# Local attention: probabilities turned by VectorE and DMA, values read by token, and a rotation's two products in one instruction

## The chip, the cores and the metric

The kernel runs on one core of one Trainium2 chip. The time is device microseconds (us) of one execution; lower is better. The core has TensorE (PE; its weight loads are shown apart as PEld), VectorE (DVE), ScalarE (ACT), GpSimd (POOL) and SyncE (SP, which here only issues DMA copies). Each engine works through its own queue in order, and they meet through semaphores.

## The reference, cut to what matters

x is 2 sequences of 1024 tokens with 128 channels. A recurrent mixing layer comes first (the first 317 us of the kernel; not touched here). Then come 6 layers of windowed attention and a gated feed-forward, with 16 heads of 64 and windows of 32 tokens:

```
def attn_layer(x, Wqkv, qs, ksc, Wo):
    q, k, v = split_heads(x @ Wqkv)
    q = l2norm(q) * qs;  k = l2norm(k) * ksc
    q = q * cos * scale + rotate_half(q) * sin * scale      # rotate_half: concat(-x2, x1)
    k = k * cos / scale + rotate_half(k) * sin / scale
    # window w of 32 queries looks at the 64 keys of windows w-1 and w
    sim = einsum('bhwie,bhwje->bhwij', bq, bk2) * 8.0
    out = einsum('bhwij,bhwje->bhwie', softmax(mask(sim)), bv2)
    return out @ Wo
```

## The kernel before, in words

The 2048 tokens are 16 blocks of 128, and 6 layers give a stream of 96 blocks, n = 0 to 95 (`STREAM`). Everything is float32 except the mask. `stream(turn)` runs 96 turns; in turn t each engine runs the stages of `turn(at, pair)` in the order in which its own `turn` function lists them. `at(lag, stage)` runs a stage for block t - lag. `pair(lag, stage)` runs a stage for a pair of two blocks, only in every other turn. So several blocks are in flight, and the order on each engine is written out by hand (lines 1307, 1479, 1668, 1832).

Two kinds of turn alternate. In an odd turn PE runs, beside the attention, `project_o` (16 matmul records of 256 columns), most of the feed-forward's matmuls and `centres`; in an even turn only `variances` and `up_gate_full`. They are called the long and the short turn below.

What a block goes through:

- `project_qk` (L1342) makes q and k in four parts of 512 columns in PSUM: q in banks 1 and 2, k in banks 0 and 1. `project_v` (L1347) makes v in two parts: part 0 in bank 2, part 1 in bank 0. Each therefore waits until the q or k part that held its bank has been read. The `rotated` semaphore says so: `rotate(n, i)` adds 3 for each part i (12 for a block), and `project_v(n, i)` waits for `6 + 3 * i`: part 0 needs rotations 0 and 1, part 1 needs rotations 0 to 2.
- `square` (ACT, L1582) squares each part; `norms` (DVE, L1768) sums the squares by head.
- `rotate(n, i)` (DVE, L1758 and L1762) multiplies part i by the cosines (512 columns into `qk`) and, in two instructions of 256 columns that cross the halves of each head, by the sines (into `turnedhalf`). GpSimd's `add_turned` (L1280) adds the two, `unit` (L1286) multiplies by the inverse norms.
- Two turns later PE turns k and q (`turn_k`, `turn_q`, L1355), ACT reads them from PSUM (L1610, L1604), PE makes the scores in banks 4 and 5 (L1390), DVE does `peaks` and `shifts` (L1774, L1781), ACT the exponential, DVE the `totals` and their reciprocals (L1788, L1790), GpSimd the division `unit_probs` (L1304).
- In the turn after that PE turns the probabilities (`turn_p`, 8 transposes of 128x128 into banks 6 and 7), ACT copies them to `p_T` (`read_p`, L1622), and PE makes the outputs (L1417) from `v_win` and `p_T` into banks 4 and 5, which ACT reads (`read_o`, L1629).
- `v_win` holds for each window the 64 value rows that it needs: `place_v` (SP, L1229 and L1231) fills it with 16 copies of 64 KB for each block.

SP also loads the next layer's weights (`load_layer`, L1207), 4 times within the stream, after `place_v` of a layer's seventh block. PE's order in a turn: `project_v(.., 1)` of the block before, `turn_k`, `turn_q`, `project_qk` 0 and 1, masks and scores, `turn_p`, (`down`), `project_qk` 2 and 3, `project_v(.., 0)`, (`project_o`), `outputs`, (`centres`). DVE's order: (`gated_full`), rotation 0, (`norm_x`), (`gated_tail`), rotation 1, `peaks`, `shifts`, (`add_ffn`), `norms` 0, rotations 2 and 3, `totals`, (`add_attention`), `norms` 1. Stages in brackets run in every other turn.

Of the kernel before, what the change touches and what calls it, by code (L numbers as in the profile page):

```python
# [28 lines left out]
P = 128  # L29
# [11 lines left out]
AH = 16  # L41
# [1035 lines left out]
LAG = 6  # L1077
PAIR = 2
# [3 lines left out]
V_SLOTS = 3  # L1082
# [4 lines left out]
def build_stream(nc, a, sems, ctx, banks, x, x_mid, early, mixed, out):  # L1087
# [49 lines left out]
    rotated, rot_added, ss_made, above_floor = sig("rotated", per=12), sig("rot_added", per=2), sig("ss_made", per=2), sig("above_floor")  # L1137
    rnorm_log, rnorm_made, qk_made, v_read = sig("rnorm_log"), sig("rnorm_made"), sig("qk_made", per=2), sig("v_read", per=2)
    v_placed = sig("v_placed", per=16 * 16)
    q_turned, qT_made, k_turned, kT_made, halo_made = sig("q_turned", per=2), sig("qT_made", per=2), sig("k_turned", per=2), sig("kT_made", per=2), sig("halo_made")  # L1140
    s_product, peak_made, shifted, exp_made = sig("s_product"), sig("peak_made", per=2), sig("shifted", per=2), sig("exp_made")
    total_made, p_normed, p_turned, pT_made = sig("total_made", per=2), sig("p_normed"), sig("p_turned", per=2), sig("pT_made", per=2)
    o_product, oT_made = sig("st_o_product"), sig("oT_made", per=2)
# [18 lines left out]
    def s_banks(n):  # L1162

        return LAST_S_BANKS if n == LAST else S_BANKS

# [53 lines left out]
    def sync(sp):  # L1219
        def place_v(n):  # L1220
            u, tok, last = n % 2, v_tok[n % V_SLOTS], v_tok[(n - 1) % V_SLOTS]
            sp.wait_ge(v_read.sem, v_read.after(n))
            sp.wait_ge(o_product.sem, o_product.after(n - 2))
            sp.wait_ge(v_placed.sem, v_placed.after(n - 1))
            for p in range(2):
                cols = slice(p * INNER // 2, (p + 1) * INNER // 2)
                for w in range(WINDOWS):
                    own, before = slice(WINDOW * w, WINDOW * (w + 1)), slice(WINDOW * (w - 1), WINDOW * w)
                    sp.dma_start(v_win[u][DH * p + WINDOW:DH * (p + 1), w, :], tok[own, cols]).then_inc(v_placed.sem, 16)  # L1229
                    src = tok[before, cols] if w else last[P - WINDOW:P, cols]  # L1230
                    sp.dma_start(v_win[u][DH * p:DH * p + WINDOW, w, :], src).then_inc(v_placed.sem, 16)  # L1231

        sp.wait_ge(cleared.sem, CLEARED)
        sp.sem_inc(v_placed.sem, v_placed.credit * v_placed.per)
# [3 lines left out]
        for n in range(BLOCKS):  # L1238
            place_v(n)
        for layer in range(1, DEPTH - 1):  # L1240
            for n in range(EARLY):
                place_v(layer * BLOCKS + n)
            sp.wait_ge(x_ready.sem, x_ready.after(layer * BLOCK_PAIRS - 1))
            sp.wait_ge(w_loaded.sem, w_loaded.after(layer))
            load_layer(sp, layer + 1, (layer + 1) % 2)
            for n in range(EARLY, BLOCKS):
                place_v(layer * BLOCKS + n)
        for n in range(BLOCKS):
            place_v((DEPTH - 1) * BLOCKS + n)
# [10 lines left out]
    def gpsimd(pool):  # L1260
# [16 lines left out]
        def add_turned(n, i):  # L1277
            half = slice(INNER * i, INNER * (i + 1))
            pool.wait_ge(rotated.sem, rotated.after(n, 6 * (i + 1)))
            nc.gpsimd.tensor_tensor(out=qk[n % 2][:, half], in0=qk[n % 2][:, half], in1=turnedhalf[:, half], op=ALU.add).then_inc(rot_added.sem, 1)  # L1280

        def unit(n, i):
            u, half = n % 2, slice(INNER * i, INNER * (i + 1))
            pool.wait_ge(rnorm_made.sem, rnorm_made.after(n))
            pool.wait_ge(rot_added.sem, rot_added.after(n, i + 1))
# [37 lines left out]
    def tensor(pe):  # L1323
        for s in (qk_product, v_product, q_turned, k_turned, s_product, p_turned, o_product, y_product, cent_product,
                  var_product, gate_product, a_product, y2_product):
            pe.sem_inc(s.sem, s.credit * s.per)
# [4 lines left out]
        def project_qk(n, i):  # L1331
# [8 lines left out]
            if i == 3:  # L1340
                pe.wait_ge(rotated.sem, rotated.after(n, 3))
# [3 lines left out]
        def project_v(n, i):  # L1345
            pe.wait_ge(rotated.sem, rotated.after(n, 6 + 3 * i))
# [12 lines left out]
        def turn_q(n):  # L1359
# [36 lines left out]
        def turn_p(n):  # L1396
            pe.wait_ge(p_normed.sem, p_normed.after(n))
            if n == LAST:
                pe.wait_ge(pT_made.sem, pT_made.after(n - 1))
            transposes(T_BANKS, p_turned, probs[n % 2][:, :, :, :].rearrange("p a b d -> p (a b d)"), kT_made, min(n + 1, STREAM - 1))  # L1400

        def outputs(n, q):

            if q == 0:
                pe.wait_ge(pT_made.sem, pT_made.after(n))
                if n < LAST - 1:
                    pe.wait_ge(shifted.sem, shifted.after(n + 1))
                elif n == LAST - 1:
                    pe.wait_ge(oT_made.sem, oT_made.after(n - 1))
                else:  # L1410
                    pe.wait_ge(shifted.sem, shifted.after(n))
                pe.wait_ge(v_placed.sem, v_placed.after(n))
            for w in range(WINDOWS):
                for side in range(2):
                    for p in range(2):
                        a_, at, rows = 2 * q + side, WINDOW * w, slice(DH * p, DH * (p + 1))
                        mm = nc.tensor.matmul(s_banks(n)[p][DH * side:DH * (side + 1), P * q + at:P * q + at + WINDOW],  # L1417
                                              v_win[n % 2][rows, w, DH * a_:DH * (a_ + 1)], p_T[rows, a_, at:at + WINDOW],
                                              start=True, stop=True, skip_group_check=True)
# [59 lines left out]
        def turn(at, pair):  # L1479
# [14 lines left out]
            at(3, turn_p)  # L1494
# [36 lines left out]
        turn_p(LAST - 2)  # L1531
        turn_q(LAST)
        up_gate_full(m - 2)
        attend(outputs, LAST - 2)
        turn_k(LAST)
        up_gate_tail(m - 2)
        masks(LAST)
        attend(scores, LAST)
        up_a_full(m - 2)
        turn_p(LAST - 1)  # L1540
        project_o(m - 1, 0)
        project_o(m - 1, 1)
        up_a_tail(m - 2)
        attend(outputs, LAST - 1)
        centres(m - 1)
        down(m - 2)
        variances(m - 1)
        turn_p(LAST)
# [21 lines left out]
    def scalar(act):  # L1570
        for s in (squared, above_floor, rnorm_log, rnorm_made, v_read, qT_made, kT_made, exp_made, pT_made, oT_made,
# [22 lines left out]
        def read_v(n, i):  # L1594
            act.wait_ge(v_placed.sem, v_placed.after(n - V_SLOTS + 1))
            act.wait_ge(v_product.sem, v_product.after(n, i + 1))
            out = v_tok[n % V_SLOTS][:, :].rearrange("p (b a d) -> p b a d", b=2, d=DH)[:, :, 4 * i:4 * i + 4, :]
            nc.scalar.activation(out, V_BANKS[i][:, :].rearrange("p (a b d) -> p b a d", b=2, d=DH), ACT.Copy).then_inc(v_read.sem, 1)
# [7 lines left out]
        def read_k(n):  # L1606
            act.wait_ge(s_product.sem, s_product.after(n - 1))
            for i in range(2):
                act.wait_ge(k_turned.sem, k_turned.after(n, i + 1))
                nc.scalar.activation(k_T[:, 4 * i:4 * i + 4, ring_at(n):ring_at(n) + P],  # L1610
                                     T_BANKS[i][:, :].rearrange("p (a t) -> p a t", a=4), ACT.Copy).then_inc(kT_made.sem, 1)
# [6 lines left out]
        def read_p(n):  # L1618
            act.wait_ge(o_product.sem, o_product.after(n - 1))
            for i in range(2):  # L1620
                act.wait_ge(p_turned.sem, p_turned.after(n, i + 1))
                nc.scalar.activation(p_T[:, 4 * i:4 * i + 4, :].rearrange("p a t -> p (a t)"), T_BANKS[i][:, :], ACT.Copy).then_inc(pT_made.sem, 1)  # L1622

        def read_o(n):
# [3 lines left out]
            for p in range(2):  # L1628
                nc.scalar.activation(o_T[:, 4 * p:4 * p + 4, at:at + P], s_banks(n)[p][:, :].rearrange("p (q t) -> p q t", t=P),  # L1629
# [38 lines left out]
        def turn(at, pair):  # L1668
# [10 lines left out]
            at(3, read_p)  # L1679
# [24 lines left out]
        read_p(LAST - 2)  # L1704
        read_q(LAST)
        exponent(LAST - 1)
        gelu_full(m - 2)
        read_o(LAST - 2)
        read_k(LAST)
        gelu_tail(m - 2)  # L1710
        logs_and_exps(m - 2)
        read_p(LAST - 1)
        exponent(LAST)
        read_o(LAST - 1)
# [3 lines left out]
        read_p(LAST)  # L1718
# [14 lines left out]
    def vector(dve):  # L1733
# [5 lines left out]
        for s in (x_ready, rotated, ss_made, peak_made, shifted, total_made, xm_made, x_normed, ff_made):  # L1739
# [5 lines left out]
        def rotate(n, i):  # L1745
# [8 lines left out]
            if i % 2 == 0:  # L1754
                dve.wait_ge(rot_added.sem, rot_added.after(n - 1, i // 2 + 1))
            cols, src = slice(512 * i, 512 * (i + 1)), by_head(QK_BANKS[i][:, :])
            cos, sin = (gains[u][:, 2 * (i // 2) + f:2 * (i // 2) + f + 1, :] for f in range(2))
            nc.vector.tensor_tensor(by_head(qk[u][:, cols]), src, cos.to_broadcast([P, 8, DH]), ALU.mult).then_inc(rotated.sem, 1)  # L1758
            half = DH // 2
            for f in range(2):  # L1760
                to, frm = slice(half * f, half * (f + 1)), slice(half * (1 - f), half * (2 - f))
                nc.vector.tensor_tensor(by_head(turnedhalf[:, cols])[:, :, to], src[:, :, frm],  # L1762
                                        sin[:, :, to].to_broadcast([P, 8, half]), ALU.mult).then_inc(rotated.sem, 1)
# [20 lines left out]
        def totals(n):  # L1784
# [5 lines left out]
            nc.vector.reciprocal(total[u][:, :], total[u][:, :]).then_inc(total_made.sem, 1)  # L1790

# [40 lines left out]
        def turn(at, pair):  # L1832
            pair(6, gated_full)
# [34 lines left out]
        m = LAST_PAIR  # L1868
        norm_x(m - 2)
# [5 lines left out]
        gated_full(m - 2)  # L1875
        totals(LAST)
        add_attention(m - 1)
        gated_tail(m - 2)
        add_ffn(m - 2)
        norm_x(m - 1)  # L1880
# [132 lines left out]
def stream_layouts(L):  # L2013
# [7 lines left out]
    wo = asn("Wo").reshape(DEPTH, PAIRS // 2, 2, 2, DH, C).transpose(0, 2, 4, 3, 1, 5)  # L2021
# [51 lines left out]
```

## Time and profile before

| what | value |
|---|---|
| median of 3 runs | 1962.6 us (1961.4 to 1962.93) |
| the profiled execution's own time | 1961.85 us |
| its span, first to last instruction | 1960.1 us |
| granted TensorE clock, mean over the span | 0.968 of full |
| the stream of 96 blocks | from 317 us to about 1885 us, then an end part up to 1949 us |
| DMA | 137.48 MB, mean 70 GB/s |

Times inside the span are counted from its first instruction. A row of the timeline gives the start, the length of the group (several instructions merged), engine, line, operation and operands, and in brackets how long the engine had been idle before it and what released it. Matmuls are pipelined, so the next one starts before the recorded end of the one before; "x128" counts records, and each float32 matmul of the outputs leaves two.

### The profile page before, as it was taken

The numbers are of one execution on the slowest core, as the hardware profiler recorded it, in microseconds if no ns is written. First come the engines' busy times: TensorE is split into PE (matmuls) and PEld (weight loads), VectorE is DVE, ScalarE is ACT, GpSimd is POOL, SyncE is SP. The second block draws the span as 40 slices with busy tenths as digits, with TensorE's granted clock in tenths as the row PEclk, the third lists the DMA queues.
The fourth block names the chain that finished last, engine by engine and source line by source line (L and its number), as shares of the span: only waits on it lengthen the run. The fifth ranks groups of instructions, "written<-read, shape, count | busy, mean of one in ns | idle before, by whom it ended". The sixth has DMA issues, their size and how long they took to land.

```text
span 1960.1 us, 75595 instructions
## 1 busy us (share of the span) xinstructions
PE 1809.8 (92%) x31926; PEld 1253.5 (64%) x31926; DVE 1488.0 (76%) x2822; ACT 1241.2 (63%) x2413; POOL 1234.4 (63%) x789
## 2 busy tenths in 40 slices
PE   7477876999999999999999999999999999999995
PEld 2144453667667667777777767677767776666773
DVE  6699947878777778787878777787878787777763
ACT  6523214577676767676767676767676767677662
POOL 3466733766666666666666666666666666666650
PEclk9799967999999999999999999999999999999996
DMA  4444002222222242222423222422224222222220
GB/s 100 123 53 56 17 3 83 63 67 67 67 66 62 68 117 71 64 72 60 122 70 73 63 67 61 125 61 72 62 70 121 70 64 69 65 67 67 66 69 22
DMA packets 89777, 137.48 MB, mean 70 GB/s; under 512 B 27168, under 2 KB 32736, under 8 KB 88416
## 3 DMA queue, kind: packets, MB, share of 16 engines
q1 hardware_dynamic: 89440, 132.66, 28.2%
q8 instruction: 252, 4.13, 0.9%
q14 instruction: 85, 0.70, 0.1%
HBM read 29.79 MB, written 2.10 MB: 16 GB/s over the span
## 4 chain that ended last, share of the span: by engine, by line
PE 49%; DVE 14%; issue 8%; POOL 6%; ACT 6%; DVEq 0%; SPq 0%; ACTq 0%; POOLq 0%; DMA 0%
PE bank L1435 8%; PE bank L1342 8%; PE bank L1417 7%; PE bank L1355 7%; PE bank L1390 5%; DVE turnedhalf L1762 5%; PE bank L1347 5%; PE bank L1452 4%; PE bank L1476 3%; POOL probs L1304 3%; DVE qk L1758 2%; POOL qk L1280 2%; DVE rnorm L1768 2%; ACT q_T L1604 1%; DVE probs L1781 1%
## 5 line engine op out<-in xcount | busy, mean ns | idle before, releaser
L1286 POOL TENSOR_TENSOR qk<-qk,rnorm 128x1024 f32<-128x1024 f32 x192 | 361.4, 1903 | 366.0 <-ACT rnorm L1592 275.4
L1280 POOL TENSOR_TENSOR qk<-qk,turnedhalf 128x1024 f32<-128x1024 f32 x192 | 454.7, 2368 | 138.8 <-DVE turnedhalf L1762 138.8
L1758 DVE TENSOR_TENSOR qk<-bank,gains 128x512 f32<-128x512 f32 x384 | 262.8, 684 | 222.0 <-ACT squares L1582 207.8
L1342 PE MATMUL bank<-wqkv,x 128*128 128x512 f32 x768 | 378.1, 596 | 4.7 <-DVE v_tok L1738 2.9
L1582 ACT ACTIVATE squares<-bank 128x512 f32<-128x512 f32 x384 | 232.6, 606 | 153.4 <-PE bank L1342 150.6
L1762 DVE TENSOR_TENSOR turnedhalf<-bank,gains 128x256 f32<-128x256 f32 x768 | 286.3, 414 | 0.0
L1629 ACT ACTIVATE o_T<-bank 128x512 f32<-128x512 f32 x192 | 104.2, 598 | 229.5 <-PE bank L1417 229.5
L1768 DVE TENSOR_REDUCE rnorm<-squares 128x16 f32<-128x1024 f32 x192 | 230.8, 1202 | 2.8
L1417 PEld LDWEIGHTS bank<-p_T,v_win 64*64 64x64 f32 x12288 | 189.9, 135 | 60.2 <-issue 57.6
L1355 PEld LDWEIGHTS bank<-st_ident,qk 128*128 128x128 f32 x1536 | 178.6, 142 | 57.1 <-issue 50.9
L1347 PE MATMUL bank<-wqkv,x 128*128 128x512 f32 x384 | 202.5, 609 | 7.0 <-DVE turnedhalf L1762 6.9
L1417 PE MATMUL bank<-p_T,v_win 64*64 64x32 f32 x12288 | 201.6, 220 | 8.0 <-issue 5.6
L1355 PE MATMUL bank<-st_ident,qk 128*128 128x128 f32 x1536 | 192.7, 274 | 0.0
L1304 POOL TENSOR_TENSOR probs<-probs,total 128x1024 f32<-128x1024 f32 x96 | 182.9, 1905 | 13.5 <-DVE total L1790 13.5
L1342 PEld LDWEIGHTS bank<-wqkv,x 128*128 128x128 f32 x768 | 138.6, 191 | 68.4 <-issue 55.1
L1435 PE MATMUL bank<-o_T,wo 128*128 128x256 f32 x768 | 173.8, 379 | 0.0
L1435 PEld LDWEIGHTS bank<-o_T,wo 128*128 128x128 f32 x768 | 145.8, 190 | 39.4 <-issue 22.0
L1452 PE MATMUL bank<-xn_T,w 128*128 128x256 f32 (+1 forms) x576 | 163.5, 393 | 7.7 <-ACT gate_T L1655 1.5
L1390 PE MATMUL bank<-k_T,q_T 64*32 64x64 f32 x12288 | 156.6, 225 | 12.8 <-issue 11.3
L1390 PEld LDWEIGHTS bank<-k_T,q_T 64*32 64x32 f32 x12288 | 136.6, 105 | 37.7 <-issue 34.0
L1808 DVE SCALAR_TENSOR_TENSOR ff_T<-bank,b,gate_T 128x256 f32<-128x256 f32 x144 | 64.7, 477 | 117.2 <-PE bank L1452 117.2
L1622 ACT ACTIVATE p_T<-bank 128x512 f32<-128x512 f32 x192 | 104.3, 594 | 75.5 <-PE bank L1355 74.4
(197 smaller groups left out, 2946.9 us busy)
## 6 DMA issues: line engine op xcount, KB each, us to landing
v_win<-v_tok SPq DMA_DIRECT2D x1536, 64.0 KB
wqkv<-in_wqkv SPq DMA_DIRECT2D x6, 1536.0 KB
v_rep_sb<-v_by_step SPq DMA_DIRECT2D x32, 128.0 KB
v_rep<-v_by_step SPq DMA_DIRECT2D x32, 128.0 KB
wo<-in_wo SPq DMA_DIRECT2D x6, 512.0 KB
w<-in_w SPq DMA_DIRECT2D x6, 341.0 KB
w<-in_w SPq DMA_DIRECT2D x6, 192.0 KB
xT_sb<-in_xT SPq DMA_DIRECT2D x1, 1024.0 KB, 4.9
```

The lines of the kernel that those rows point to most:

```text
L1280: nc.gpsimd.tensor_tensor(out=qk[n % 2][:, half], in0=qk[n % 2][:, half], in1=turnedhalf[:, half], op=ALU.add).then_inc(rot_added.sem, 1)
L1286: nc.gpsimd.tensor_tensor(out=by_head(qk[u][:, half]), in0=by_head(qk[u][:, half]), in1=rnorm[u][:, AH * i:AH * (i + 1)].unsqueeze(2).to_b ...
L1342: nc.tensor.matmul(QK_BANKS[i][:, :], shifted_tokens(x, n, P), layer_cols(wqkv, n, 3 * INNER, 512 * i, 512), start=True, stop=True).then_i ...
L1347: nc.tensor.matmul(V_BANKS[i][:, :], shifted_tokens(x, n, P), layer_cols(wqkv, n, 3 * INNER, 2 * INNER + 512 * i, 512), start=True, stop=T ...
L1355: mm = nc.tensor.transpose(outs[i // 4][:, P * (i % 4):P * (i % 4 + 1)], source[:, P * i:P * (i + 1)], ident[:, :])
L1390: mm = nc.tensor.matmul(s_banks(n)[p][at:at + WINDOW, 2 * WINDOW * a_:2 * WINDOW * (a_ + 1)], q_T[rows, a_, at:at + WINDOW], k_T[rows, a_, ...
L1417: mm = nc.tensor.matmul(s_banks(n)[p][DH * side:DH * (side + 1), P * q + at:P * q + at + WINDOW], v_win[n % 2][rows, w, DH * a_:DH * (a_ + ...
L1435: mm = nc.tensor.matmul(ff_bank(m)[:, 0:PT], layer_cols(wo, n, INNER, C * i, C), o_T[:, i, :], start=(i == 0), stop=(i == PAIRS - 1))
L1452: mm = nc.tensor.matmul(ff_bank(m)[0:size, PT * j:PT * (j + 1)], layer_cols(w1, PAIR * m, 2 * FF, at + f0, size), xn_T[:, :], start=True, ...
L1758: nc.vector.tensor_tensor(by_head(qk[u][:, cols]), src, cos.to_broadcast([P, 8, DH]), ALU.mult).then_inc(rotated.sem, 1)
L1762: nc.vector.tensor_tensor(by_head(turnedhalf[:, cols])[:, :, to], src[:, :, frm], sin[:, :, to].to_broadcast([P, 8, half]), ALU.mult).then ...
L1768: nc.vector.reduce_sum(rnorm[n % 2][:, AH * h:AH * (h + 1)], by_head(squares[:, INNER * h:INNER * (h + 1)]), AX).then_inc(ss_made.sem, 1)
```

## The change

Three things change in the stream.

**Probabilities.** PE's `turn_p` and ACT's `read_p` go. DVE's new `turn_p`, first in its turn, transposes 32x32 blocks of the probabilities (128x1024 in all) into `p_blocks`, and SP's `place_p` copies them in 8 copies of 64 KB to `p_T` (now two buffers). `place_p(n - 2)` is issued ahead of `place_v(n)`. **Values.** `v_win` goes; the outputs read `v_tok` itself for odd windows and `v_shift`, the same rows moved down by 32, for even windows; `place_v` is 2 copies (384 KB and 128 KB) in place of 16. The outputs' matmuls keep number and size (64 of 64x64 by 32 columns) but go to banks 6 and 7 in another order, and `turn_k`, no longer `turn_q`, waits for `read_o` of two blocks before. **Rotation.** One DVE instruction makes both products of a part (1024 results from 512 values), and `add_turned` crosses the halves, in 4 instructions of 512 columns for a block in place of 2 of 1024. `rotated` now counts 4 for a block, one for each part. The end part's order is rewritten to suit.

```diff
-    rotated, rot_added, ... = sig("rotated", per=12), sig("rot_added", per=2), ...
+    rotated, rot_added, ... = sig("rotated", per=4), sig("rot_added", per=4), ...
 SP
         def place_v(n):
...
+            sp.dma_start(v_shift[u][WINDOW:P, :], tok[0:P - WINDOW, :]).then_inc(v_placed.sem, 16)
+            sp.dma_start(v_shift[u][0:WINDOW, :], last[P - WINDOW:P, :]).then_inc(v_placed.sem, 16)
+        def place_p(n):
+            sp.wait_ge(p_turned.sem, p_turned.after(n))
+            sp.wait_ge(o_product.sem, o_product.after(n - 2))
+            sp.wait_ge(p_placed.sem, p_placed.after(n - 1))
+            for w in range(WINDOWS):
+                for half in range(2):
+                    row = DH * (w // 2) + WINDOW * half
+                    sp.dma_start(p_T[n % 2][row:row + WINDOW, w % 2, :, :], p_blocks[WINDOW * w:WINDOW * (w + 1), half, :, :]).then_inc(p_placed.sem, 16)
+        def place(n):
+            if n >= LAG_P:
+                place_p(n - LAG_P)
+            place_v(n)
 GpSimd
         def add_turned(n, i):
+            part = slice(INNER * i, INNER * (i + 1))
+            pool.wait_ge(rotated.sem, rotated.after(n, 2 * (i + 1)))
+            for f in range(2):
+                to, frm = slice(half * f, half * (f + 1)), slice(half * (1 - f), half * (2 - f))
+                out = by_head(qk[n % 2][:, part])[:, :, to]
+                nc.gpsimd.tensor_tensor(out=out, in0=out, in1=by_head(turned[:, part])[:, :, frm], op=ALU.add).then_inc(rot_added.sem, 1)
 TensorE
             if i == 3:
-                pe.wait_ge(rotated.sem, rotated.after(n, 3))
+                pe.wait_ge(rotated.sem, rotated.after(n, 1))
         def project_v(n, i):
-            pe.wait_ge(rotated.sem, rotated.after(n, 6 + 3 * i))
+            pe.wait_ge(rotated.sem, rotated.after(n, 3 + i))
         def turn_q(n):
-                transposes(S_BANKS, q_turned, qk[n % 2][:, 0:INNER], oT_made, n - 2)
+                transposes(S_BANKS, q_turned, qk[n % 2][:, 0:INNER], shifted, n - 1)
         def turn_k(n):
-            transposes(T_BANKS, k_turned, qk[n % 2][:, INNER:2 * INNER], pT_made, n - 2)
+                transposes(T_BANKS, k_turned, qk[n % 2][:, INNER:2 * INNER], oT_made, n - 2)
-        def turn_p(n):
-            pe.wait_ge(p_normed.sem, p_normed.after(n))
-            transposes(T_BANKS, p_turned, probs[n % 2][:, :, :, :].rearrange("p a b d -> p (a b d)"), kT_made, min(n + 1, STREAM - 1))
         def outputs(n, q):
+            for a_ in (2 * q, 2 * q + 1):
+                for turn_ in range(2):
+                    v = v_tok[n % V_SLOTS] if turn_ else v_shift[n % 2]
+                    for g in range(2):
+                        for p in range(2):
+                            rows, head = slice(DH * g, DH * (g + 1)), 2 * a_ + p
+                            at = DH * a_ + WINDOW * turn_
+                            mm = nc.tensor.matmul(o_banks(n)[g][DH * p:DH * (p + 1), at:at + WINDOW], v[rows, DH * head:DH * (head + 1)],
+                                                  p_T[n % 2][rows, turn_, head, :], start=True, stop=True, skip_group_check=True)
 ScalarE
-        def read_p(n):
...
 VectorE
         def rotate(n, i):
+            both = rot[:, u:u + 2, cols].rearrange("p f (h d) -> p f h d", d=DH)
+            pair_of_gains = gains[u][:, 2 * (i // 2):2 * (i // 2) + 2, :]
+            nc.vector.tensor_tensor(both, src.unsqueeze(1).to_broadcast([P, 2, 8, DH]), pair_of_gains.unsqueeze(2).to_broadcast([P, 2, 8, DH]),
+                                    ALU.mult).then_inc(rotated.sem, 1)
+        def turn_p(n):
+            dve.wait_ge(p_normed.sem, p_normed.after(n))
+            dve.wait_ge(p_placed.sem, p_placed.after(n - 1))
+            nc.vector.transpose(p_blocks[:, :, :, :], probs[n % 2][:, :, :, :].rearrange("t a p (g k) -> t g (a p) k", k=WINDOW)).then_inc(p_turned.sem, 1)
         def turn(at, pair):
+            at(3, turn_p)
             pair(6, gated_full)
```

## Rows read from the trace of the kernel before

**Rows 1.** The page, part 1: busy time, share of the span, instructions.

```profile
PE 1809.8 (92%) x31926; PEld 1253.5 (64%) x31926; DVE 1488.0 (76%) x2822; ACT 1241.2 (63%) x2413; POOL 1234.4 (63%) x789
```

**Rows 2.** Busy time by stretch (length, PE, PEld, DVE, ACT, POOL, clock, DMA, GB/s).

```profile
1004.42:1023.53 19.11, 19.00 (x331) 13.87 (x327) 16.81 (x32) 11.71 (x24) 13.84 (x8) 1.00 0.23 57
1023.53:1036.89 13.36, 13.36 (x303) 9.31 (x301) 9.02 (x18) 11.64 (x23) 8.54 (x6) 1.00 0.34 82
```

**Rows 3.** Timeline: ACT's square once a pair; first, two steady ones, last.

```profile
394.81 0.38 ACT L1635 ACTIVATE cent_sq<-bank 128x256 f32<-128x256 f32 x1 [1.65 <-PE bank L1442]
...
992.15 0.39 ACT L1635 ACTIVATE cent_sq<-bank 128x256 f32<-128x256 f32 x1
1024.37 0.39 ACT L1635 ACTIVATE cent_sq<-bank 128x256 f32<-128x256 f32 x1
...
1884.72 0.39 ACT L1635 ACTIVATE cent_sq<-bank 128x256 f32<-128x256 f32 x1
```

**Rows 4.** Timeline, PE: value projection to outputs, long turn, then short turn.

```profile
1016.79 1.02 PE L1347 MATMUL bank<-wqkv,x 128*128 128x512 f32 x2
...
1017.65 3.62 PE L1435 MATMUL bank<-o_T,wo 128*128 128x256 f32 x16
...
1021.20 2.07 PE L1417 MATMUL bank<-p_T,v_win 64*64 64x32 f32 x128
...
1033.94 1.02 PE L1347 MATMUL bank<-wqkv,x 128*128 128x512 f32 x2
...
1034.89 2.07 PE L1417 MATMUL bank<-p_T,v_win 64*64 64x32 f32 x128
```

**Rows 5.** Timeline, DVE: rotation 2 of the long turn; then the short turn.

```profile
1018.62 0.75 DVE L1762 TENSOR_TENSOR turnedhalf<-bank,gains 128x256 f32<-128x256 f32 x2
...
1028.37 0.69 DVE L1758 TENSOR_TENSOR qk<-bank,gains 128x512 f32<-128x512 f32 x1 [4.34 <-ACT squares L1582]
...
1029.64 0.41 DVE L1800 TENSOR_TENSOR xn<-bank,rstd 128x256 f32<-128x256 f32 x1
...
1033.62 1.21 DVE L1768 TENSOR_REDUCE rnorm<-squares 128x16 f32<-128x1024 f32 x1
...
1034.74 0.68 DVE L1758 TENSOR_TENSOR qk<-bank,gains 128x512 f32<-128x512 f32 x1
1035.34 0.74 DVE L1762 TENSOR_TENSOR turnedhalf<-bank,gains 128x256 f32<-128x256 f32 x2
```

**Rows 6.** Timeline, PE: value projection of the stream's first block.

```profile
325.76 1.12 PE L1347 MATMUL bank<-wqkv,x 128*128 128x512 f32 x2 [1.26 <-DVE turnedhalf L1762]
```

**Rows 7.** Timeline, long turn: from the outputs' reading to rotation 1.

```profile
1005.31 1.08 ACT L1629 ACTIVATE o_T<-bank 128x512 f32<-128x512 f32 x2
...
1008.42 1.03 PE L1452 MATMUL bank<-xn_T,w 128*128 128x256 f32 x4
...
1009.48 0.88 DVE L1808 SCALAR_TENSOR_TENSOR ff_T<-bank,b,gate_T 128x256 f32<-128x256 f32 x2 [2.01 <-PE bank L1452]
...
1012.08 0.69 DVE L1758 TENSOR_TENSOR qk<-bank,gains 128x512 f32<-128x512 f32 x1
```

**Rows 8.** Timeline, GpSimd, the same long turn.

```profile
1005.06 2.37 POOL L1280 TENSOR_TENSOR qk<-qk,turnedhalf 128x1024 f32<-128x1024 f32 x1 [0.80 <-DVE turnedhalf L1762]
...
1007.39 1.90 POOL L1304 TENSOR_TENSOR probs<-probs,total 128x1024 f32<-128x1024 f32 x1
...
1009.25 0.74 POOL L1273 TENSOR_TENSOR gains<-tables,qk_gain 128x256 f32<-128x256 f32 x1
```

**Rows 9.** Timeline, PE: the probabilities' transposes.

```profile
1012.84 1.09 PE L1355 MATMUL bank<-st_ident,probs 128*128 128x128 f32 x8
```

**Rows 10.** Timeline of SP's queue: one value copy issued.

```profile
1001.46 0.59 SPq L1231 DMA_DIRECT2D v_win<-v_tok  x1
```

**Rows 11.** DMA issues: a 64 KB load, with microseconds to landing.

```profile
masks_f<-in_mask SPq DMA_DIRECT2D x1, 64.0 KB, 1.9
```

**Rows 12.** Busy time while a layer's weights load (columns as in rows 2).

```profile
706.00:720.50 14.50, 12.79 (x302) 9.12 (x301) 11.03 (x22) 11.78 (x22) 10.74 (x7) 1.00 0.87 264
```

**Rows 13.** Timeline, end part: the last block's outputs on PE.

```profile
1913.65 2.07 PE L1417 MATMUL bank<-p_T,v_win 64*64 64x32 f32 x128 [2.20 <-ACT p_T L1622]
```

More of the change, by code:

```diff
@@ L1224, in place_v @@
             sp.wait_ge(v_placed.sem, v_placed.after(n - 1))
[L1225 to L1231, printed above, removed]
+            sp.dma_start(v_shift[u][WINDOW:P, :], tok[0:P - WINDOW, :]).then_inc(v_placed.sem, 16)
[12 more added lines that the diff above has]
+            place_v(n)
         sp.wait_ge(cleared.sem, CLEARED)
-        sp.sem_inc(v_placed.sem, v_placed.credit * v_placed.per)
+        for s in (v_placed, p_placed):
+            sp.sem_inc(s.sem, s.credit * s.per)
         sp.wait_ge(w_loaded.sem, w_loaded.after(0))
@@ L1238, in sync @@
         for n in range(BLOCKS):
-            place_v(n)
+            place(n)
         for layer in range(1, DEPTH - 1):
             for n in range(EARLY):
-                place_v(layer * BLOCKS + n)
+                place(layer * BLOCKS + n)
             sp.wait_ge(x_ready.sem, x_ready.after(layer * BLOCK_PAIRS - 1))
@@ L1246, in sync @@
             for n in range(EARLY, BLOCKS):
-                place_v(layer * BLOCKS + n)
-        for n in range(BLOCKS):
-            place_v((DEPTH - 1) * BLOCKS + n)
+                place(layer * BLOCKS + n)
+        for n in range(BLOCKS - 1):
+            place((DEPTH - 1) * BLOCKS + n)
+        place_p(LAST - 2)
+        place_p(LAST - 1)
+        place_v(LAST)
+        place_p(LAST)
         def store(n0, n1):
@@ L1284, in unit @@
             pool.wait_ge(rnorm_made.sem, rnorm_made.after(n))
-            pool.wait_ge(rot_added.sem, rot_added.after(n, i + 1))
+            pool.wait_ge(rot_added.sem, rot_added.after(n, 2 * (i + 1)))
             nc.gpsimd.tensor_tensor(out=by_head(qk[u][:, half]), in0=by_head(qk[u][:, half]),
@@ L1411, in outputs @@
                     pe.wait_ge(shifted.sem, shifted.after(n))
+                pe.wait_ge(v_read.sem, v_read.after(n))
                 pe.wait_ge(v_placed.sem, v_placed.after(n))
[L1413 to L1419, printed above, removed]
+                pe.wait_ge(p_placed.sem, p_placed.after(n))
+            for a_ in (2 * q, 2 * q + 1):
[7 more added lines that the diff above has]
+                                                  p_T[n % 2][rows, turn_, head, :], start=True, stop=True, skip_group_check=True)
             if q == QUARTERS - 1:
@@ L1530, in tensor @@
         attend(scores, LAST - 1)
-        turn_p(LAST - 2)
         turn_q(LAST)
         up_gate_full(m - 2)
-        attend(outputs, LAST - 2)
         turn_k(LAST)
-        up_gate_tail(m - 2)
         masks(LAST)
         attend(scores, LAST)
+        up_gate_tail(m - 2)
+        attend(outputs, LAST - 2)
         up_a_full(m - 2)
-        turn_p(LAST - 1)
+        up_a_tail(m - 2)
         project_o(m - 1, 0)
         project_o(m - 1, 1)
-        up_a_tail(m - 2)
+        down(m - 2)
+        centres(m - 1)
         attend(outputs, LAST - 1)
-        centres(m - 1)
-        down(m - 2)
         variances(m - 1)
-        turn_p(LAST)
         attend(outputs, LAST)
@@ L1717, in scalar @@
         affine(m - 1)
-        read_p(LAST)
+        read_o(LAST - 1)
         read_o(LAST)
@@ L1754, in rotate @@
             if i % 2 == 0:
-                dve.wait_ge(rot_added.sem, rot_added.after(n - 1, i // 2 + 1))
+                dve.wait_ge(rot_added.sem, rot_added.after(n - 1, 2 * (i // 2 + 1)))
             cols, src = slice(512 * i, 512 * (i + 1)), by_head(QK_BANKS[i][:, :])
[L1757 to L1763, printed above, removed]
+            both = rot[:, u:u + 2, cols].rearrange("p f (h d) -> p f h d", d=DH)
+            pair_of_gains = gains[u][:, 2 * (i // 2):2 * (i // 2) + 2, :]
+            nc.vector.tensor_tensor(both, src.unsqueeze(1).to_broadcast([P, 2, 8, DH]), pair_of_gains.unsqueeze(2).to_broadcast([P, 2, 8, DH]),
+                                    ALU.mult).then_inc(rotated.sem, 1)
         def norms(n, h):
@@ L1868, in vector @@
         m = LAST_PAIR
+        turn_p(LAST - 2)
         norm_x(m - 2)
@@ L1875, in vector @@
         gated_full(m - 2)
+        turn_p(LAST - 1)
+        gated_tail(m - 2)
         totals(LAST)
         add_attention(m - 1)
-        gated_tail(m - 2)
         add_ffn(m - 2)
+        turn_p(LAST)
         norm_x(m - 1)
@@ L2020, in stream_layouts @@
     out["wqkv"] = np.ascontiguousarray(asn("Wqkv"))
-    wo = asn("Wo").reshape(DEPTH, PAIRS // 2, 2, 2, DH, C).transpose(0, 2, 4, 3, 1, 5)
+    wo = asn("Wo").reshape(DEPTH, PAIRS, P, C).transpose(0, 2, 1, 3)
     out["wo"] = np.ascontiguousarray(wo.reshape(DEPTH, P, INNER))
@@ L2045, in stream_layouts @@
     for s in (scale, f(1.0) / scale):
-        parts += [cos * s, cos * s, -sin * s, sin * s]
-    tab = np.concatenate(parts, 1).astype(f)
+        parts += [np.concatenate([cos * s, cos * s], 1), np.concatenate([sin * s, -sin * s], 1)]
+    tab = np.stack(parts, 1).astype(f).reshape(SEQ_BLOCKS, P, 2, 2, DH)
+    tab[1::2] = tab[1::2, :, :, ::-1].copy()
     out["tables"] = np.ascontiguousarray(tab.reshape(SEQ_BLOCKS, P, 4 * DH).transpose(1, 0, 2))
```

72 lines of the change are left out of this document (33 added, 39 removed).

## The prediction, made before the changed kernel was run

> **What bounds the kernel now.** I read the page's busy shares first: PE 92%, DVE 76%, ACT and POOL 63% each [rows 1]. That alone points at PE, but the share is an average, so I next took the busy time of two neighbouring turns: the long turn lasts 19.11 us with PE busy for 19.00, DVE 16.81, the short one 13.36 us with PE at 13.36, DVE 9.02, ACT 11.64 [rows 2]. A busy PE here is partly modelled, so the chain of waits and the timeline decide. They show one loop per pair of turns, in which PE is on the path for only about half. After a long turn's outputs end, ACT works through its reads, and DVE's first rotation waits 4.34 us for it; DVE then runs to the end of the short turn's rotations; GpSimd adds and divides; DVE's gating product follows, and from there PE runs without a gap to the end of the long turn's outputs. The pair takes 1024.37 - 992.15 = 32.2 us there (32.48 in the neighbouring pairs), and (1884.72 - 394.81) / 45 = 33.1 us on average over 45 pairs [rows 3]. The excess of 0.6 is PE waiting for instructions here and there. The granted clock is 1.00 in the stretches read, the upper of its two levels (2.4 GHz), though PE has short gaps near the weight loads [rows 2, 12].
>
> **The part that decides: one wait moved by one rotation.** Before, `project_v` part 0 waits for count 6 of 12, which is rotations 0 and 1. After, the count is 4 per block, one per rotation, and the wait is `3 + i`: part 0 waits for rotations 0, 1 and 2, part 1 for all four. Keeping the meaning would have been `2 + i`. Bank 2 holds q's second half, so rotation 1 is all that the data needs; the third is an extra. Rotation 2 comes on DVE after `peaks`, `shifts`, `norms` 0 (and `add_ffn`), and behind the waiting projection on PE stand `project_o` and the outputs, for which ACT, and through it the next turn's DVE, wait. That such a wait shows as PE idleness can be seen in the stream's first block: 1.26 us before part 1, released by a rotation [rows 6].
>
> Short turn. Before, part 0 starts at 1033.94 [rows 4], while rotation 2 ends at 1035.34 + 0.74 = 1036.08 [rows 5]. The new rotation is one instruction of 1024 results. Its step from start to next start I take from the reduction over 1024 columns, 1034.74 - 1033.62 = 1.12, against 1.27 for a rotation now (1028.37 to 1029.64) [rows 5], say 1.14. Three rotations save 3 x 0.13 = 0.4, so rotation 2 ends at 1035.7, and the projection starts 1.8 us later than before. The outputs follow at once, also 1.8 later.
>
> From there into the long turn. ACT's read of the outputs began at 1005.31, 0.8 us after they ended, because ACT was busy with the gate; that slack is absorbed, so ACT is late by 1.1, and PE by 1.8. The gating product on DVE (1009.48, released by PE [rows 7]) comes about 1.5 later (bounds 1.1 and 1.8), and rotation 1, which stands at 1012.08 and is held by ACT's square, about 1.4 later.
>
> Long turn. After rotation 1 DVE works without a gap to rotation 2, which ended at 1018.62 + 0.75 = 1019.37 [rows 5]. It now ends at 1019.37 + 1.4 - 2 x 0.14 = 1020.5. The projection was at 1016.79 [rows 4] and now starts at 1020.5: 3.75 us later. `project_o` and the outputs take as long as before (6.5 us from projection to end [rows 4]), so the pair grows by 3.75. Bounds: 2.8 if DVE's instructions overlap more than I think and the first delay carries over only at 1.1, 5.2 if the new rotation costs as much as four quarters with GpSimd beside it (1.5 us each) and nothing is absorbed. Of the 0.6 us of scattered PE waits in the mean pair some fall into the new gaps: I take off 0.3. With 47 pairs: 47 x 3.45 = 162 us.
>
> **The other parts, which this wait covers.** PE loses 8 transposes, 1.09 us a block [rows 9], and ACT its two reads. Both lie before the new wait: PE only waits longer, worth 0. Without the cover they would give back about 1.0 us per pair, in the long turn, where PE is on the path. DVE gains `turn_p`: 1024 elements, no such instruction in the trace; nearest is the reduction of the same size, 1.21 [rows 5]; bounds 0.7 (half) and 2.4 (two passes). I take 1.2. It waits for GpSimd's division, which ended at 1007.39 + 1.90 = 1009.29 [rows 8], 0.2 before the gating product. With rotations 0.5 us earlier and the adds 0.2 longer it is ready at 1009.0, turned at 1010.2, and the gating product now comes at 1011.0: 0.8 us to spare. Behind it on DVE stand gating and rotation 0, and PE waits for the gating. At 2.4 us it would cost 0.4 a pair. In the short turn DVE idles 4.34 us there [rows 5].
>
> GpSimd's adds: four of 512 columns. From 2.37 for 1024 and 0.74 for 256 [rows 8] a line gives 0.2 + 2.12 per 1000 columns, 1.28 for 512, +0.2 us per half. Halves of 32 columns might run slower; bounds 0 and +1.4. Up to +1.0 is hidden, as shown.
>
> The probabilities' way: 8 copies at 0.63 us from start to start (0.59 each [rows 10]) are 5.0 us, landing 1.9 after the last (nearest: a 64 KB load [rows 11]; bounds 1 and 4). In the long turn they are there by about 1010.2 + 5.0 + 1.9 = 1017.1, the outputs start at 1025; in the short turn about 5 us are to spare. Worth 0. SP's queue is `place_p`, then `place_v`, which waits for the same turn's outputs; values are needed two turns later. `turn_k` now waits for `read_o`: PE gets there after `project_v` part 1 (0.9 us), when ACT has half of it; 0 to 0.5, I take 0.1, inside the rounding.
>
> The exception is a layer's load. It is issued behind a long turn's `place_v`, which now ends 1.2 us after the outputs; the engines are then busy at 0.87 for 14.5 us [rows 12], and the probabilities for that short turn's outputs are issued behind it. They would land about 17 to 19 us after the turn's start instead of 8, where the outputs want them at 13.4. Four times 4 us = 16 (bounds 0 and 24). On this the Trainium skill (DMA: Bandwidth & Descriptors, "Queues, rings and completion order") says that SP owns one ring on each of the 16 engines and that descriptors are consumed in ring order. By that rule the full 4 us apply; if copies shared the engines evenly it would be near 0. No row of the kernel before shows which.
>
> End part: two blocks' probabilities now reach PE over DVE, 8 issues and a landing (8.1 us) instead of 2.2 (transposes and reads); the last one already stood 2.20 us before the outputs [rows 13]. I take +6, bounds 0 and 12.
>
> **The sum.** On the profiled execution's own 1961.85 us (span 1960.1, the rest around it; 0.75 below the median of 1962.6): 1961.85 + 162 + 16 + 6 = 2146 us.
>
> **The rivals.**
> A. The outputs' matmuls run slower. Neighbouring matmuls now share their 64 rows and alternate columns, where they alternated rows. At 2.07 us for 128 records [rows 4] they plainly overlap, and if half of that is lost, each turn grows by 2.07: 96 x 2.07 = 199 more, 2345. For it: the order does change. Against: all four quarters of the array are still used in turn, and each row half still has its own bank. 8%.
> B. VectorE's transpose or GpSimd's halves are slow: at 2.4 us, or +1.4 per half, the gating product is late by 0.4 to 0.7 more; 47 x 0.5 = 24, 2170. 12%.
> The Trainium skill (VectorE: DVE Perf Modes, "The three transpose paths") gives 311 ns for 128x128 in bf16 on VectorE; eight of these would be an estimated 2.5 us, which is this rival's case. The Trainium skill (Vector Engine (DVE) Microarchitecture Reference, "The reshape front-end and per-opcode configuration") says that the transpose sustains one element per cycle and lane. No run here shows yet which of the two holds.
> C. The other side: the wait is met before PE arrives, so the change does what its parts promise. It decides at the point where rotation 2 ends before PE reaches the projection; DVE would have to be 1.8 us earlier in the short turn and 2.5 in the long. Then per pair: rotations -0.52, `turn_p` and its place before the gating +0.96, adds +0.2, transposes -1.02, together -0.4; 48 x -0.4 = -18, with the end part +6: 1950. Against it: halving every rotation would bring only 1.9. 5%.
> D. Only the short turn's delay or only part of the long one's survives, because the orders overlap otherwise than I chained them: growth 2 per pair, 94 + 22: 2078. 10%.
>
> **How the numbers follow.** Forecast 65%, A 8, B 12, C 5, D 10. Range 2075 to 2232: lower end 47 x 2.3 + 5, upper end 47 x 5.2 + 26. It holds the forecast, B and D. Slower by over 0.2% (4 us, about what can be told from no change): forecast, A, B, D, less a remainder: 94%; within: 1%; faster: 5%.
>
> **What would show it.** In the profile after: the value projection on PE idle 1.5 to 4 us before it, released by the rotation, in every turn; pairs of about 36; PE's share down to about 83%; long turn's DVE idle before `add_attention`, which waits for `project_o`. The single rotation should read 1.2 us, the transpose 1.2, an add 1.3. The prediction is wrong if the projection shows no idle time, or if the outputs' group takes more than 2.5 us.

## The result, and the profile after

The changed kernel takes 2315.69 us (median of 4 runs, 2310.28 to 2320.16) against 1962.0 us before: the ratio is 1.181, with a 95% interval of 1.178 to 1.184. I forecast slower, at 2146 us, and a range up to 2232. The direction and the place are right; the size is not, and the time lies outside the range.

The page after, parts 1 and 2 (busy shares; tenths of the granted clock in 40 slices):

```profile
PE 1914.3 (83%) x31158; PEld 1270.6 (55%) x31158; DVE 1557.5 (67%) x2150; ACT 1149.4 (50%) x2221; POOL 1256.3 (54%) x981
...
PEclk9799788989999889889998988888988999898997
```

PE has 768 matmul records fewer than in [rows 1] and is busy for 105 us more. So the same matmuls take longer than they did before, and something other than waiting happened. The granted clock says what: 0.898 over the span instead of 0.968, with 8s (tenths, cut off) throughout the stream.

The wait is where the prediction put it. Timeline of PE after, one short turn and the long one behind it:

```profile
1263.64 1.53 PE L1379 MATMUL bank<-wqkv,x 128*128 128x512 f32 x2 [1.91 <-DVE rot L1777]
1265.10 0.44 PE L1450 MATMUL bank<-p_T,v_shift 64*64 64x32 f32 x8
...
1268.32 0.42 PE L1450 MATMUL bank<-p_T,v_tok 64*64 64x32 f32 x8
1268.67 2.07 PE L1379 MATMUL bank<-wqkv,x 128*128 128x512 f32 x2
...
1284.29 1.69 PE L1379 MATMUL bank<-wqkv,x 128*128 128x512 f32 x2 [2.85 <-DVE rot L1777]
1285.78 4.78 PE L1467 MATMUL bank<-o_T,wo 128*128 128x256 f32 x16
```

L1379 is `project_v`. Part 0 stands 1.91 us in the short turn and 2.85 in the long one, released by the rotation, where it had no idle time in [rows 4]. Behind it the work is slow: part 1 takes 2.07 us for what took 1.02, `project_o` 4.78 for 3.62, and the short turn's outputs (L1450, from 1265.10 to 1268.74) 3.64 for 2.07. Stretches of that pair show why (columns as in rows 2; the clock is the third figure from the end):

```profile
1264.20:1271.10 6.90, 6.90 (x135) 4.80 (x134) 4.22 (x5) 2.89 (x6) 5.49 (x5) 0.51 0.18 46
1271.00:1281.00 10.00, 9.89 (x167) 6.63 (x165) 6.10 (x10) 6.34 (x13) 3.31 (x2) 1.00 0.29 81
1281.00:1284.30 3.30, 0.45 (x3) 0.01 (x1) 3.21 (x5) 1.82 (x3) 2.89 (x3) 1.00 0.00 0
1284.70:1288.15 3.45, 3.45 (x8) 2.26 (x7) 2.05 (x3) 0.00 (x0) 2.70 (x3) 0.51 0.02 5
```

In this pair the clock is whole while PE is idle, and within 0.6 us of PE's going on it falls to about half (1.2 GHz, the lower level): 0.51 over 6.90 us in the short turn and 0.51 over 3.45 in the long one. Then it is whole again. In other turns it fell up to 0.9 us before PE went on. Not every idle time brings it. By the granted clock of the trace it fell around the projection in 29 of the 45 short turns and 28 of the 45 long ones, and the length of the idle time doesn't tell them apart: the median is 1.91 us in short turns with a fall and without, and 2.85 in long ones with and without. The pairs that hold 1.00 take 36.7 to 37.6 us, the usual pair with both falls 41.4. The same stretch view of one pair of each:

```profile
604.78:641.49 36.71, 31.32 (x611) 21.33 (x610) 27.23 (x35) 21.30 (x43) 22.74 (x17) 1.00 0.22 59
1252.25:1293.65 41.40, 36.11 (x611) 24.41 (x610) 27.13 (x35) 21.41 (x42) 22.75 (x17) 0.88 0.20 53
```

The mean of 45 pairs, between the first and the last but two of ACT's squares that come once a pair, is (2235.39 - 406.83) / 45 = 40.63 us against the 33.11 of [rows 3].

### The profile page after: what moved, and what is told of

Same layout as the page of the kernel before. It is cut to its first block, busy times and chain, and to the rows that moved or that the text cites. A ratio compares the mean times of both kernels' runs of the same rounds, so it can differ in the third digit from the quotient of the medians.

```text
span 2315.2 us, 72907 instructions
## 1 busy us (share of the span) xinstructions
PE 1914.3 (83%) x31158; PEld 1270.6 (55%) x31158; DVE 1557.5 (67%) x2150; ACT 1149.4 (50%) x2221; POOL 1256.3 (54%) x981
## 4 chain that ended last, share of the span: by engine, by line
PE 44%; DVE 29%; issue 12%; DMA 6%; ACT 3%; SPq 2%; DVEq 1%; POOL 0%; ACTq 0%; POOLq 0%
PE bank L1450 10%; DVE rot L1777 10%; PE bank L1379 9%; PE bank L1467 9%; PE bank L1387 5%; DMA v_shift<-v_tok 4%; PE bank L1484 3%; DVE probs L1796 3%; DVE rnorm L1783 3%; DVE peak L1789 3%; PE bank L1374 2%; PE bank L1425 2%; DVE ff_T L1829 2%; DVE x L1850 2%; DVE sc_ub L671 1%
## 5 line engine op out<-in xcount | busy, mean ns | idle before, releaser
L1318 POOL TENSOR_TENSOR rot<-rot,rnorm 128x1024 f32<-128x1024 f32 x192 | 361.0, 1901 | 737.1 <-ACT rnorm L1620 717.6
L1777 DVE TENSOR_TENSOR rot<-bank,gains 128x1024 f32<-128x1024 f32 x384 | 458.4, 1215 | 191.6 <-ACT squares L1610 190.1
L1312 POOL TENSOR_TENSOR rot<-rot 128x512 f32<-128x512 f32 x384 | 477.0, 1264 | 98.6 <-DVE rot L1777 98.6
L1379 PE MATMUL bank<-wqkv,x 128*128 128x512 f32 x384 | 267.3, 785 | 230.6 <-DVE rot L1777 230.6
L1450 PE MATMUL bank<-p_T,v_shift 64*64 64x32 f32 x6144 | 233.2, 244 | 19.7 <-DMA p_T<-p_blocks 12.5
L1450 PEld LDWEIGHTS bank<-p_T,v_shift 64*64 64x64 f32 x6144 | 197.8, 162 | 84.9 <-issue 84.9
L1379 PEld LDWEIGHTS bank<-wqkv,x 128*128 128x128 f32 x384 | 69.3, 214 | 317.9 <-DVE rot L1777 312.5
L1387 PEld LDWEIGHTS bank<-st_ident,rot 128*128 128x128 f32 x1536 | 196.3, 154 | 78.8 <-issue 73.5
L1450 PE MATMUL bank<-p_T,v_tok 64*64 64x32 f32 x6144 | 230.4, 242 | 1.5 <-issue 1.5
L1387 PE MATMUL bank<-st_ident,rot 128*128 128x128 f32 x1536 | 210.6, 290 | 0.4 <-DVE probs L1796 0.2
L1450 PEld LDWEIGHTS bank<-p_T,v_tok 64*64 64x64 f32 x6144 | 199.2, 163 | 3.2 <-issue 3.2
L1811 DVE STREAM_TRANSPOSE p_blocks<-probs 128x1024 f32<-128x1024 f32 x96 | 119.0, 1240 | 94.6 <-POOL probs L1336 94.6
```

The source lines that it names most:

```text
L1312: nc.gpsimd.tensor_tensor(out=out, in0=out, in1=by_head(turned[:, part])[:, :, frm], op=ALU.add).then_inc(rot_added.sem, 1)
L1318: nc.gpsimd.tensor_tensor(out=by_head(qk[u][:, half]), in0=by_head(qk[u][:, half]), in1=rnorm[u][:, AH * i:AH * (i + 1)].unsqueeze(2).to_b ...
L1379: nc.tensor.matmul(V_BANKS[i][:, :], shifted_tokens(x, n, P), layer_cols(wqkv, n, 3 * INNER, 2 * INNER + 512 * i, 512), start=True, stop=T ...
L1387: mm = nc.tensor.transpose(outs[i // 4][:, P * (i % 4):P * (i % 4 + 1)], source[:, P * i:P * (i + 1)], ident[:, :])
L1450: mm = nc.tensor.matmul(o_banks(n)[g][DH * p:DH * (p + 1), at:at + WINDOW], v[rows, DH * head:DH * (head + 1)], p_T[n % 2][rows, turn_, he ...
L1777: nc.vector.tensor_tensor(both, src.unsqueeze(1).to_broadcast([P, 2, 8, DH]), pair_of_gains.unsqueeze(2).to_broadcast([P, 2, 8, DH]), ALU. ...
```

## The experiments

Eight kernels were run. Theory W holds the moved wait responsible, with the fall of the clock behind it; the rivals hold the probabilities' way, the order of the outputs, or the load of a layer.

**a_wait: the wait mended.**

```diff
-            pe.wait_ge(rotated.sem, rotated.after(n, 3 + i))
+            pe.wait_ge(rotated.sem, rotated.after(n, 2 + i))
```

> The changed kernel with project_v waiting for count 2 + i instead of 3 + i; all else as changed. Theory W (the rotation too many in this wait, with the drop of TensorE's granted clock that its idle time brings, is the whole loss): PE's idle time before the value projection goes, the clock of a pair returns to 1.00, and the time is that of my rival C, 1950 us (1930 to 1985). Rival P (the way of the probabilities over VectorE and DMA, or the new order of the output matmuls, holds the loop or takes the clock down by itself): the time stays above 2100 us, and PE's idle time moves to the outputs, released by the copies of p_T or by read_o.

Measured: 1978.11 us, ratio to before 1.007 (1.0045 to 1.009), mean clock 0.954. One digit was worth 338 us. The usual pair takes 32.13 us, against 32.48 before, so the rest of the change shortens it by 0.35 us; rival C's sum gave 0.4. Still the kernel is not faster: four times a pair takes 39.5 to 40.5 us, and the end part is 10.7 us longer. My 1950 had neither the four pairs nor the whole of the end part.

**b_late: only the wait moved, in the kernel before.**

```diff
-            pe.wait_ge(rotated.sem, rotated.after(n, 6 + 3 * i))
+            pe.wait_ge(rotated.sem, rotated.after(n, 9 + 3 * i))
```

> The kernel before with only this wait moved by one rotation: 9 + 3 * i of 12. Theory W: the loss is there without any other part of the change. The old rotation ends 0.4 us later in the short turn and the transposes of the probabilities still stand on PE, so about 8 us a pair instead of 7.5: 2330 us (2290 to 2380), granted clock under 0.92. Rival P: at most the 3.5 us a pair that I forecast, without a fall of the clock, 2100 to 2140 us, the rest of the loss being the other parts'.

Measured: 2257.72 us, ratio 1.15 (1.144 to 1.156), clock 0.938. The wait alone costs 293 us against the 1965.2 of the kernel before in the same rounds, well over the 138 to 178 of rival P, and less than I expected. The clock fell less often here, in 12 of 45 short turns and 21 of 45 long ones. Many pairs hold 1.00 and take 37.4 us, others are far longer at a mean of 0.96:

```profile
600.73:641.62 40.89, 35.20 (x627) 24.23 (x626) 25.87 (x48) 23.48 (x46) 22.22 (x13) 0.96 0.22 54
846.06:883.41 37.35, 33.09 (x627) 23.12 (x626) 25.78 (x48) 23.46 (x46) 22.33 (x13) 1.00 0.24 59
```

The clock is not all of that difference: in the first of these pairs a scores matmul stood 1.15 us and an output matmul 0.94 us for no recorded reason. PE still has the probabilities' transposes here, and its idle time before the projection is shorter in the long turn (2.27 us in the median, against 2.85) but not in the short one (2.00, against 1.91). Why the clock falls less often is not shown.

**a_fed, a_fed_short, a_fed_long: the late wait kept, PE kept busy in it.**

```diff
         def project_v(n, i):
+            if i == 0:
+                pe.wait_ge(kT_made.sem, kT_made.after(n - 2))
+                for _ in range(3 if n % 2 else 2):
+                    nc.tensor.matmul(T_BANKS[0][:, :], ...512 columns of wqkv..., start=True, stop=True)
             pe.wait_ge(rotated.sem, rotated.after(n, 3 + i))
```

In a_fed_short the count is `0 if n % 2 else 2`, in a_fed_long `3 if n % 2 else 0`.

> The changed kernel with its late wait kept, and ahead of it, in each turn, matmuls of 512 columns into bank 6, whose results nobody reads: 2 in the short turn (about 1.7 us of the 1.9 idle) and 3 in the long one (2.6 of 2.9). Theory W-clock (about half of the loss is not the waiting but the half clock after it): the waits stay nearly as long counted from rotation to projection, but the granted clock stays near 0.97, the pair falls from 40.6 to about 37 us and the time to 2150 us (2120 to 2185). Rival (the clock falls for another reason, or the time is lost only by waiting): no change or slower, 2300 to 2330 us.

> The changed kernel with its late wait, and the unread matmuls ahead of it in short turns only (2 of 512 columns). Theory (each idle time takes the clock down for the stretch behind it; the short turn's idle time of 1.9 us costs the outputs and the next block's projection and transposes, the long one's 2.9 us costs project_o): about half of the 128 us come back, 2250 us (2225 to 2280), and the clock is low only behind the long turn's wait. Rival (the clock answers to the mean load of the pair, not to one idle time): the time stays over 2290 us or falls by all of it.

> The same with the unread matmuls in long turns only (3 of 512 columns). Theory: the other half comes back, 2250 us (2225 to 2280), the clock low only behind the short turn's wait. Rival: over 2290 us, or all of it. What the two runs gain should add up to the 128 us of the kernel with both.

Measured: 2187.95 us with both (ratio 1.115, 1.110 to 1.120; clock 0.963), 2253.57 with the short turns fed (two runs; 1.1475, 1.144 to 1.151), 2236.23 with the long turns fed (two runs; 1.139, 1.1355 to 1.142). More work made the kernel 128 us faster. The gains, 62 and 79 us, add up to 141, about the 128. So each of the two idle times brings falls of its own: in a_fed the clock fell around none of the 90 projections, in a_fed_short around 34 of the 45 long turns' and none of the short ones', in a_fed_long around 19 of the 45 short turns' and none of the long ones'. The timeline and the pair's stretch of a_fed:

```profile
1131.21 1.12 PE L1384 MATMUL bank<-wqkv,x 128*128 128x512 f32 x2 [0.20 <-DVE rot L1782]
...
1148.93 1.13 PE L1384 MATMUL bank<-wqkv,x 128*128 128x512 f32 x2 [0.34 <-DVE rot L1782]
1149.89 3.62 PE L1472 MATMUL bank<-o_T,wo 128*128 128x256 f32 x16
```

```profile
1119.82:1156.61 36.79, 35.67 (x621) 23.20 (x620) 27.23 (x35) 21.30 (x43) 22.90 (x17) 1.00 0.23 59
```

The projections start as late as ever, `project_o` is back at 3.62 us, and the pair takes what an unfed pair without a fall takes. Where only one turn is fed, the clock is low behind the other: in a_fed_short behind the long turn's wait, in a_fed_long behind the short turn's.

```profile
978.00:991.73 13.73, 10.86 (x154) 7.48 (x153) 9.66 (x13) 3.11 (x5) 9.20 (x8) 0.88 0.01 2
```

```profile
457.00:467.00 10.00, 9.53 (x152) 7.24 (x151) 4.04 (x5) 5.03 (x12) 5.05 (x4) 0.66 0.27 74
```

I had expected 2150 for both; a_fed's mean pair is 37.7 us, not 37. Most of that is the four pairs at a layer's load, 41.1 to 44.5 us, in which PE waits 2.8 to 3.7 us for the probabilities' copies; the other 41 take 37.2 in the mean.

**b_rot: the rotation's part alone.** The kernel before, with the new `rotate` and `add_turned` as in the diff above, the buffer and tables that they need, and its waits with their old meaning (`2 + i`).

> The kernel before with the rotation's part alone: one VectorE instruction for both products, halves crossed in GpSimd's four additions, all waits with their old meaning. From the trace after (a rotation 1.18 us from start to start against 1.27, four additions of 1.26 against two of 2.37): VectorE gains 0.09 x 4 a turn, GpSimd loses 0.1 a half, the path keeps about 0.3 a pair: 1948 us (1935 to 1962). Rival: the additions of strided halves delay the probabilities by more than VectorE gains, 1965 us or more.

Measured: 1960.36 us, ratio 0.997 (0.994 to 0.999): faster by 0.3%, less than the expected 0.7%, and the rival is out. In the profiled execution (1963.0 us) the usual pair stays at 32.5 us and the mean pair is 33.17, so the trace doesn't show where the 0.3% comes from. That VectorE is not alone on the path would explain the unchanged pair; it is not shown.

**a_spread: the layers' weights in parts.** a_wait, and (the comments are added here):

```diff
-            load_layer(sp, layer + 1, (layer + 1) % 2)
             for n in range(EARLY, BLOCKS):
+                if n - EARLY < len(SPREAD):            # ((0, 1), (2, 3), (4,), (5, 10), (6, 7), (8,), (9,))
+                    for part in SPREAD[n - EARLY]:     # 11 parts: wqkv in 6, wo in 2, w1, w2, qk_gain
+                        load_part(sp, layer + 1, (layer + 1) % 2, part)
                 place(layer * BLOCKS + n)
```

> The changed kernel with project_v's wait of the old meaning (2 + i), and each layer's weights loaded in 11 parts of at most 341 KB over seven turns, instead of 5 loads in one go ahead of the probabilities' copies. Theory L (with the wait mended, what keeps the change slower than before is the probabilities queued behind a layer's load: pairs of 40.0 us where the others take 32.1, four times, and the end part): the four long pairs go back to 32 to 33.5 us and the time falls by 4 x 7 = 28 us, to 0.993 of before (0.989 to 0.997). Rival (the long pairs come from something else at a layer's start, such as loading code or the first block's mask): they stay at 38 us or more and the time within 5 us of the 1978 us of the mended kernel.

Measured: 1947.53 us, ratio 0.992 (0.989 to 0.994), 31 us less than a_wait. VectorE's turning, SP's queue and the outputs of a_wait at a load, and then the pairs at the same load in a_wait and in a_spread:

```profile
688.40 0.67 SPq L1218 DMA_DIRECT2D wqkv<-in_wqkv  x1
...
689.23 1.25 DVE L1811 STREAM_TRANSPOSE p_blocks<-probs 128x1024 f32<-128x1024 f32 x1 [1.08 <-POOL probs L1336]
...
691.25 1.10 SPq L1219 DMA_DIRECT2D qk_gain<-in_qk_gain  x1
692.45 5.00 SPq L1248 DMA_DIRECT2D p_T<-p_blocks  x8
...
703.84 0.44 PE L1450 MATMUL bank<-p_T,v_shift 64*64 64x32 f32 x8 [5.38 <-DMA p_T<-p_blocks]
```

```profile
688.13:728.13 40.00, 34.13 (x611) 24.20 (x610) 27.11 (x35) 21.61 (x42) 22.96 (x18) 0.87 0.43 124
```

```profile
692.80:724.86 32.06, 31.04 (x611) 21.52 (x610) 26.99 (x34) 21.14 (x43) 23.00 (x18) 1.00 0.36 102
```

PE waited 5.38 us for the probabilities' copies and then ran at the lower clock, so a wait of 5.4 us made the pair 7.9 us longer. The lateness has two parts. The probabilities were turned by 690.48, but SP was issuing the load until 692.35, which is 2.0 us. And the copies landed 11.4 us after the first was issued, 6.4 after the last, where 5 us of issue and about 2 of landing had been forecast. With the load in parts the pair is like all others. The Trainium skill (DMA: Bandwidth & Descriptors, "Queues, rings and completion order") says that on each DMA engine SP's descriptors are consumed in ring order. The trace agrees: the load's last part, issued at 691.25, landed 11.0 us later, at about 702.3, and the copies behind it at 703.84.

**a_best: the end part's order.** a_spread, with `turn_p` of the last two blocks ahead of `gated_full` and `add_ffn` on VectorE, and `totals(LAST)` ahead of `gated_tail`.

> The same with VectorE's order in the end part changed: the last two blocks' probabilities turned ahead of the gating and of the feed-forward's addition. Theory: each stands 1 us earlier at SP's queue and the end part, 10 us longer than before, loses 1 to 2 us: 2 us faster than the kernel with the loads spread alone (0 to 4). Rival: the gating that now waits takes back what the turning gains, no difference.

Measured: 1943.84 us, ratio 0.990 (0.988 to 0.992). Its interval overlaps a_spread's, so the times alone don't show the 3.7 us between them. The two traces have the 45 pairs alike (32.50 and 32.49 us) and the end part at 85.9 and 80.8 us, which speaks for the new order. It is the fastest version run, and 1% under the kernel before.

## Why the prediction was right in direction and wrong in size

- **The moved wait: right in its place, too small in its size.** The idle time was forecast from rotation 2's end at 1.8 us (short turn) and reads 1.91; the long turn's is 2.85. At the whole clock the pair shown grew by 36.7 - 32.5 = 4.2 us; I had 3.75, and 3.45 after taking off 0.3 for scattered PE waits. In a_fed, where the clock holds except at the loads, the mean pair is 37.72 - 33.11 = 4.61 us longer than before. Over 45 pairs that is 207 us: 22 in the four pairs at a load, 185 in the others, where the forecast has 155 for 45 pairs.
- **The step that failed: "`project_o` and the outputs take as long as before (6.5 us from projection to end [rows 4])".** In the long turn shown they take 8.3 us (1284.29 to the outputs' end at 1292.56). The step rested on the granted clock of 1.00 read in a kernel whose PE hardly stood still, and took that clock as given. The wait itself changed it: behind many of its idle times of 1.9 and 2.9 us PE ran at 1.2 GHz for several microseconds, on the path. After less a_fed, 40.63 - 37.72 = 2.91 us a pair, is 131 us. No term of the sum and no rival had it, and it alone takes the time beyond the range: a_fed's 2188 lies within it.
- **The sum again, with what was measured:** the wait with the rest of the change, loads included, 207, the clock 131, the first pairs 12 (406.8 less 394.8), the end part 4 (79.8 less 75.4, forecast 6): 354 us, the spans' difference being 355. The forecast was 162 + 16 + 6 = 184.
- **The layer's load: mechanism right.** I had 4 us for each, from rows that didn't show the copies. With the wait mended it is 7.9, of which 5.4 are the wait. In the changed kernel itself the outputs come later, and the four pairs (44.8, 43.3, 43.9 and 44.3 us) are 3.8 us longer than the mean of the others (40.3). In three of them PE waited 2.3 to 3.1 us for the copies; in the fourth a scores matmul stood 3.2 us for no recorded reason.
- **Two signs of mine that mislead.** PE's share came out at the forecast 83% by luck: its busy time grew by 105 us at the lower clock, and the span by 355. And I had said that outputs of more than 2.5 us would prove the prediction wrong, meaning rival A. They took 3.64 in the short turn shown, but from the clock, not from their order.
- **VectorE's transpose:** 1.24 us forecast at 1.2; rival B is out, and with it the 2.5 us estimated from the Trainium skill (VectorE: DVE Perf Modes, "The three transpose paths"). The Trainium skill (Vector Engine (DVE) Microarchitecture Reference, "The reshape front-end and per-opcode configuration") has the transpose at one element per cycle and lane. The trace fits that: 1024 results in a lane take 1.24 us as a transpose, 1.21 as a reduction and 1.22 as a multiplication. The rotation reads 1.22 (forecast 1.2), an addition 1.26 (1.3). What leaving out PE's transposes and ACT's two reads gives back by itself was not measured.
- **Rival A, slower outputs: out.** At the whole clock the 128 records take 2.07 us in the long turn shown (1290.49 to 1292.56), the 2.07 of [rows 4]; at the lower clock they take the 3.64 above.
- **Rival C's price:** the loop's part, -0.4 a pair, came out (-0.35); its end part was 10.7 us, not 6, and the loads were not in it. Its condition never held.

## What to carry to other kernels

When semaphore counts are renumbered, translate each wait into the event it stands for; `6 + 3 * i` of 12 is `2 + i` of 4, and one rotation more cost 338 us. When a wait is added on TensorE, price the work behind it at both clock levels, not only at the clock of the old trace (here the lower one added 131 us to the 207). If the wait must stay, unread matmuls in it can pay for themselves. A copy that becomes urgent should not stand in a queue behind a bulk load: split the load.

## What the runs showed of the hardware

TensorE's clock fell to half behind idle times of 1.9 and 2.9 us, in a loop where it was busy for over 80% of the time: after 1.91 us of idleness it was at 0.51 over 6.9 us. The same idle times did not always bring it: it fell around 57 of 90 projections, the idle times being equally long with a fall and without, and what decides between the two is left open. With the idle time filled by matmuls that nobody reads, down to 0.2 and 0.3 us, it fell around none of 90. The Trainium skill (TensorE: Matmul & The Clock Gate, "HAM oscillation — how this bites in real kernels") describes such an alternation of idle time and half clock for a loop that waits for DMA. The runs agree that idle time on TensorE is followed by the half clock; here the releaser is VectorE, and the idle times are shorter than the DMA waits of some 3 to 5 us which that section gives.
